# Two mixture-of-experts stages: the first-layer and gate biases move into the weights' last row, and VectorE adds the second-layer bias

## The reference

```python
logits = x @ gate_w.T + gate_b                   # 8 experts
top_vals, top_idx = top_k(logits, 2)
for e in range(8):
    h = x @ w1[e].T + b1[e]                      # 2 x 256 columns
    y = h[:, 0::2] * sigmoid(1.702 * h[:, 0::2]) * (h[:, 1::2] + 1.0)
    out += (y @ w2[e].T + b2[e]) * we[:, None]   # we: routing weight of expert e
```

## Time and profile before

| | |
|---|---|
| runs, us | 1161.66, 1163.23, 1166.33 (median 1163.23) |
| span of the profiled execution, first to last instruction, us | 1142.1 |
| mean granted TensorE clock | 0.931 |
| busy, share of the span | PE 90%, PEld 74%, DVE 64%, ACT 39%, POOL 38% |
| moved by DMA | 72.49 MB, mean 63 GB/s |

### The profile page before, as it was taken

The page is one execution under the profiler, slowest core; times in us unless marked ns, Lnnn a source line. Parts: engine busy times, 40 slices in busy tenths (PEclk is TensorE's granted clock), DMA queues, the critical chain, the costliest instruction groups (busy, mean ns, idle before and its releaser), DMA issues. The chain is left out here.

```text
span 1142.1 us, 18339 instructions
## 1 busy us (share of the span) xinstructions
PE 1029.9 (90%) x6327; PEld 844.4 (74%) x6327; DVE 732.0 (64%) x1755; ACT 449.2 (39%) x768; POOL 430.7 (38%) x473
## 2 busy tenths in 40 slices
PE   4889995879999999978999987999988998899997
PEld 3778884756566655568878886888877987788886
DVE  7935442899788876647454445756648978456654
ACT  4324331327576654525343322232325543232222
POOL 3046663337363721203556531000129987300000
PEclk8689998889899997896999998999998999999999
DMA  9024422400000010119452241000010120000000
GB/s 335 37 74 139 171 88 83 128 0 2 2 2 20 2 39 20 39 37 352 149 189 89 79 174 53 1 1 1 1 74 1 28 47 1 1 1 19 20 19 19
DMA packets 39339, 72.49 MB, mean 63 GB/s; under 512 B 10642, under 2 KB 28114, under 8 KB 38996
## 3 DMA queue, kind: packets, MB, share of 16 engines
q1 hardware_dynamic: 29460, 48.25, 12.6%
q0 software_dynamic: 7680, 20.98, 5.6%
q10 hardware_dynamic: 2112, 2.10, 0.5%
HBM read 47.04 MB, written 24.13 MB: 62 GB/s over the span
## 5 line engine op out<-in xcount | busy, mean ns | idle before, releaser
L2139 PE MATMUL ps<-xt,w 128*128 128x512 f32 x768 | 191.3, 399 | 7.5 <-PEq L66 7.5
L2139 PEld LDWEIGHTS ps<-xt,w 128*128 128x128 f32 x768 | 142.4, 191 | 37.0 <-issue 5.8
L1822 DVE CUSTOM_DVE_ANT_0 ps<-ps,att_mask 128x128 f32<-128x128 f32 (+3 forms) x256 | 119.2, 515 | 27.2 <-PE ps L1371 26.9
L717 PE MATMUL ps<-moe_w,moe_narrow_xb 128*128 x480 | 127.6, 402 | 0.0
L2233 DVE TENSOR_TENSOR had_gated<-ps,had_sig 128x512 f32<-128x512 f32 x64 | 44.2, 691 | 109.7 <-ACT had_sig L2192 109.7
L2192 ACT ACTIVATE had_sig<-ps 128x512 f32<-128x512 f32 x64 | 38.2, 597 | 188.4 <-PE ps L2139 188.4
L1679 ACT ACTIVATE att_early_probs<-ps 128x384 f32<-128x384 f32 (+1 forms) x192 | 91.2, 528 | 52.1 <-PE ps L1386 51.5
L122 POOL TENSOR_TENSOR var_eps<-bn,eps 128x4 f32<-128x4 f32 x24 | 6.6, 274 | 277.0 <-DVE bn L99 263.0
L621 POOL DMA_INDIRECT made_rows<-moe_units_made,moe_index x80 | 79.4, 993 | 80.4 <-ACT moe_units_made L844 68.3
L615 POOL DMA_INDIRECT moe_xs<-xn_rows,moe_index x80 | 79.3, 991 | 76.0 <-DVE moe_index L1016 44.1
L717 PEld LDWEIGHTS ps<-moe_w,moe_narrow_xb 128*128 128x128 f32 x480 | 92.0, 192 | 20.2
(11 more groups left out here) (286 smaller groups left out, 2242.8 us busy)
## 6 DMA issues: line engine op xcount, KB each, us to landing
moe_w<-in_moe SPq DMA_DIRECT2D x16, 768.0 KB, 8.9
back<-made_rows SPq DMA_DIRECT2D x16, 512.0 KB, 5.4
x<-x_turned SPq DMA_DIRECT2D x8, 512.0 KB, 8.6
low_weights<-moe_w SPq DMA_DIRECT2D x4, 768.0 KB, 3.6
moe_w<-low_weights SPq DMA_DIRECT2D x4, 768.0 KB, 15.2
x<-in_x SPq DMA_DIRECT2D x4, 512.0 KB, 5.5
xn_rows<-moe_wide_xn SPq DMA_DIRECT2D x4, 512.0 KB, 10.6
moe_narrow_later<-in_w SPq DMA_DIRECT2D x4, 512.0 KB, 4.6
```

Of the source, the lines that this page charges most:

```text
L717: last = nc.tensor.matmul(h_bank(j, i), xb[a][:, j % 2, i, k, :], weight(c), start=False, stop=(k == KC - 1 and c == 1))
L1822: last = nc.vector.tensor_tensor_reduce(g.ps[:, a, col:col + n], g.ps[:, a, col:col + n], mask[:, SEQ - n:SEQ], -1.0, 3.0e38, ALU.add, ALU ...
L2139: last = nc.tensor.matmul(g.ps[:, bank(n, half), :], w[a][:, k, c * P:(c + 1) * P], xt[low][:, b % 2, k, :], start=(k == 0 and q == 0), st ...
```

## The change

In both expert layers the normalised rows keep 255 columns, and the last is set to 1.0 (by POOL in stage 0; ahead of stage 1 by one small DVE memset for each of the four batches). Since the 256 values add up to zero, the last row of a weight matrix can be subtracted from all the others, and the last row then holds the bias.

- w1: POOL subtracts the last row (broadcast in `w1_last`) from each record, two tensor_tensor of 128 x 512 an expert (`shift_w1`). In stage 0 the last rows are broadcast by four DMAs of 512 KB each (`last_rows`); in stage 1 by products with a column of the identity and four ACT copies.
- b1: PE turns it into `b1_rows`, ACT copies it out, and SP puts row e over the last row of record e by a small DMA (`place_b1`), which waits for the record. `high(e)` waits for the shift and for the placed row.
- Stage 0 shifts all eight experts and stores high and low parts of experts 4 to 7; stage 1 shifts only 0 to 3 and loads both parts of 4 to 7. That is twelve records' worth into SBUF in stage 1, as before.
- gate: `gate_b` becomes the last row of `gate_w`, POOL subtracts the old last row (`shift_gates`); `choose` copies instead of adding.
- b2 is broadcast to all partitions (1 MB), and `out` moves from ACT to DVE: two tensor_tensor of 128 x 256, b2 chosen by a register. `gated` has one buffer instead of two.
- The bias products, `bias_rows` and the tiles for them go away.

The diff, cut:

```diff
+LAST_ROW = slice(REC_W1 - 2 * I, REC_W1)
...
+            def place_b1(e):
+                sp.wait_ge(b1_out, 1)
+                sp.wait_ge(rec_here[e], 16)
+                sp.dma_start(f32(w[1][P - 1:P, e, LAST_ROW]), b1_rows[e:e + 1, :]).then_inc(b1_placed[e], 16)
+            def stored_split(e):
+                sp.dma_start(f32(w[0][:, e, :]), g.split_dram[0, e - E // 2]).then_inc(rec_here[e], 16)
+                sp.dma_start(f32(w[1][:, e, :]), g.split_dram[1, e - E // 2]).then_inc(low_here[e], 16)
+            def last_rows(q):
+                sp.dma_start(w1_last[:, 2 * q:2 * q + 2, :],
+                             ins["moe"][2 * q:2 * q + 2, P - 1, LAST_ROW].partition_broadcast(P)).then_inc(last_here[q], 16)
...
             if which == 0:
...
+                first_biases()
                 for e in range(E // 2):
+                    if e % 2 == 0:
+                        last_rows(e // 2)
                     record(e)
                 for b in range(BATCH):
                     sp.wait_ge(norm.xn_done, b + 1)
                     sp.dma_start(by_tiles(g.xn_dram[:, :], b), g.xn[:, b, :, :]).then_inc(xn_stored, 16)
+                    if b % 2 == 0:
+                        last_rows((E // 2 + b) // 2)
                     record(E // 2 + b)
+                    place_b1(b)
+                for e in range(E // 2, E):
+                    place_b1(e)
+                second_biases()
             else:
+                sp.dma_start(last_row[:, :], ins["moe"][0:OWN, P - 1, LAST_ROW]).then_inc(last_here[0], 16)
+                first_biases()
+                for e in range(OWN):
+                    record(e)
+                for e in range(OWN, E):
+                    stored_split(e)
+                for e in range(OWN):
+                    place_b1(e)
+                second_biases()
...
+                nc.gpsimd.memset(g.xn[:, :, :, D - 1:D], 1.0)
+                norm.rstd(pool, 0)
+                shift_gates()
+                norm.rstd(pool, 1)
+                norm.rstd(pool, 2)
+                shift_w1(0)
+                shift_w1(1)
+                norm.rstd(pool, 3)
+                for e in range(2, E):
+                    shift_w1(e)
...
-                    nc.tensor.matmul(h_bank(j, i), owner_row[:, n:n + 1].to_broadcast([P, P]), b1_row[:, :],
-                                     start=True, stop=False)
...
-                    nc.tensor.matmul(O_BANK[:, i * D:(i + 1) * D], owner_row[:, n:n + 1].to_broadcast([P, P]),
-                                     b2_row[:, :], start=(i == 0), stop=False, skip_group_check=True)
...
             def high(e):
-                act.wait_ge(rec_here[e], 16)
+                act.wait_ge(w1_shifted, e + 1)
+                act.wait_ge(b1_placed[e], 16)
...
                 high_norm(1)
-                high(0)
                 choice.out_of_gates(act, 0, 2)
-                high(1)
+                out_b1(1)
                 high_norm(2)
+                high(0)
                 choice.out_of_gates(act, 1, 3)
+                high(1)
                 high(2)
                 high_norm(3)
...
+            def out(j):
+                mine = [nc.vector.value_load(owner_i[0:1, 2 * j + i:2 * j + i + 1], min_val=0, max_val=E - 1)
+                        for i in range(2)]
+                dve.wait_ge(o_ready, j + 1)
+                if j >= 2:
+                    dve.wait_ge(scattered[j % 2], 32 * (j // 2))
+                for i in range(2):
+                    last = nc.vector.tensor_tensor(made[:, j % 2, i, :], O_BANK[:, i * D:(i + 1) * D],
+                                                   b2[:, bass.ds(mine[i], 1), :], ALU.add)
+                last.then_inc(out_done, 1)
...
                 if 1 <= j <= PAIRS:
                     low_y(j - 1)
+                if j >= 2:
+                    out(j - 2)
                 if 0 <= j - 2 < len(jobs):
                     low_later(j - 2)
```

More of the change, by code:

```diff
@@ L404, in experts_stage @@
         sem = Semaphores(nc, ctx, tag)
-        w = [sb(f"w{q}", [P, E, REC_W1 + REC_W2], F32R) for q in range(2)]
+        w = [sb(f"w{q}", [P, E, REC], F32R) for q in range(2)]
+        b2 = sb("b2", [P, E, D])
         if which == 0:
@@ L462, in experts_stage @@
         xb = [narrow(f"xb{q}", [P, 2, 2, KC, P], F32R) for q in range(2)]
-        gated = narrow("gated", [P, 2, 2, IC, P])
+        gated = narrow("gated", [P, 2, IC, P])
+        sig = narrow("sig", [P, 2, IC, P])
         later = narrow("later", [P, HID])
         consts, small_here, b2_here = sem("consts"), sem("small_here"), sem("b2_here")
+        last_here = [sem(f"last_here{q}") for q in range(4 if which == 0 else 1)]
+        b1_here, b1_turned, b1_out = sem("b1_here"), sem("b1_turned"), sem("b1_out")
+        b1_placed = [sem(f"b1_placed{e}") for e in range(E if which == 0 else E // 2)]
+        last_ps, last_out, w1_shifted, gate_shifted = sem("last_ps"), sem("last_out"), sem("w1_shifted"), sem("gate_shifted")
         x_here = [sem(f"x_here{b}") for b in range(BATCH)]
@@ L635, in _, with turn_b1 @@
         def _(pe):
-            def turn_biases():
-                pe.wait_ge(b1_filled, 1)
+            def turn_b1(bank):
+                pe.wait_ge(b1_here, 16)
                 for q in range(2 * IC):
-                    last = nc.tensor.transpose(Y_BANK[:, q * P:(q + 1) * P], b1_src[:, q, :], g.ident[:, :])
+                    last = nc.tensor.transpose(g.ps[0:E, bank, q * P:(q + 1) * P], b1_all[:, :, q], g.ident[:, :])
                 last.then_inc(b1_turned, 1)
+            if which == 1:
+                turn_b1(LAST_BANKS[0])
+                pe.wait_ge(last_here[0], 16)
+                for e in reversed(range(OWN)):
+                    if e == 0:
+                        pe.wait_ge(b1_out, 1)
+                    nc.tensor.matmul(g.ps[:, LAST_BANKS[e], :], g.ident[0:OWN, e:e + 1].to_broadcast([OWN, P]),
+                                     last_row[:, :], start=True, stop=True).then_inc(last_ps, 1)
             if which == 0:
@@ L683, in _ @@
             if which == 1:
-                pe.wait_ge(lo_split, E - LOADED)
+                pe.wait_ge(lo_split, OWN)
                 spin(nc, g, 4, 6)
-            pe.wait_ge(hi_split, E)
-            pe.wait_ge(lo_split, E - LOADED)
-            if which == 1:
-                for e in range(E - LOADED, E):
-                    pe.wait_ge(low_here[e], 16)
-            pe.wait_ge(b_row, 2)
+            pe.wait_ge(hi_split, OWN)
+            pe.wait_ge(lo_split, OWN)
+            for e in range(OWN, E):
+                pe.wait_ge(rec_here[e], 16)
+                pe.wait_ge(low_here[e], 16)
             pe.wait_ge(owner_done, 1)
@@ L810, in _ @@
                 high(7)
-                high_biases()
                 routes()
             else:
+                out_b1(LAST_BANKS[0])
+                for e in reversed(range(OWN)):
+                    act.wait_ge(last_ps, OWN - e)
+                    nc.scalar.activation(w1_last[:, e, :], g.ps[:, LAST_BANKS[e], :], ACT.Copy).then_inc(last_out, 1)
                 routes()
-                for e in range(E):
+                for e in range(OWN):
                     high(e)
-                high_biases()
                 act.wait_ge(route_turned, 1)
@@ L838, in high_y @@
                 nc.scalar.activation(yb[0][:, j % 2, :, :, :], Y_BANK, ACT.Copy).then_inc(yhi_done, 1)
-            def out(j):
-                act.wait_ge(o_ready, j + 1)
-                if j >= 2:
-                    act.wait_ge(scattered[j % 2], 32 * (j // 2))
-                nc.scalar.activation(made[:, j % 2, :, :], O_BANK, ACT.Copy).then_inc(out_done, 1)
             def high_later(j):
@@ L942, in _ @@
             nc.vector.memset(count[:, 3, :], 1.0)
-            if which == 0:
-                bias_rows()
             padded, ends, starts = count[:, 0, :], count[:, 1, :], count[:, 2, :]
@@ L1024, in _ @@
             dve.wait_ge(routed, 23)
-            nc.vector.tensor_copy(owner_i[:, :], owner[:, :])
-            nc.vector.tensor_scalar(owner_row[:, :], owner[:, :], g.row_e[:, :], None, ALU.is_equal) \
-                .then_inc(owner_done, 1)
-            if which == 1:
-                bias_rows()
-            for e in range(E if which == 0 else 3, E - LOADED):
+            nc.vector.tensor_copy(owner_i[:, :], owner[:, :]).then_inc(owner_done, 1)
+            for e in range(E if which == 0 else 3, OWN):
                 low_weights(e)
```

165 lines of the change are left out of this document (75 added, 90 removed).

## The result

The changed kernel takes 1197.09 us (median of 4 runs, 1190.91 to 1201.79) against 1162.45 of the kernel before beside it: ratio 1.0275, 95% interval 1.0241 to 1.0309. It is **slower by 35 us**, outside the range of the forecast. The profiled execution took 1201.79 us, the slowest of the four; its span is 1199.7.

The account below looks back on a forecast made before the run. Loops were taken as bound by PE's instruction stream, prologues by DMA and the chain through ACT and DVE. Terms -26.1 + 10.1 + 14 + 0.7 = -1.3 gave 1162 us from the median 1163.23; range 1151 to 1171.

Parts of the forecast that it names:

- The loops: Both stages' loops: forty pairs without bias products gain 28.0 us, less 0.5 for POOL and 1.4 for a stall: -26.1.
- the 5.08: Both loops: forecast period of one pair in us without the bias products, down from 5.78.
- what I had named as able to take over: Loops at the new period: POOL's transfers (5.1 us a pair), DVE (4.2) or PE's wait for `low_x` (0.27 away).
- The stall for later weights: Stage 1's loop: ACT's 4.64 us stand for a transfer of later weights grows, giving 1.4 us back.
- POOL's 5.1 a pair: Loops: POOL's four indirect transfers take 5.1 us a pair, level with PE; 0.5 us taken off the gain.
- Stage 0's prologue: Before stage 0's loop: broadcasts delay record 6 and b1's placement, so the last choice ends at 47.7 against 37.58, +10.1 us.
- my chain: Stage 0's prologue: after ACT's 1.48, DVE's three splits, one low part and four choices run without a gap, 10.8 us.
- the upper bound: Stage 0's prologue: +14 us if the chain's three splits each stood behind one POOL shift, +3.6.
- Stage 1's prologue: Before stage 1's loop: b1 placements queue behind all twelve records in SP's queue, delaying the third split and index, +14 us.
- Overtaking: Faster rival, chance 0.20: placements overtake the records, stage 1's prologue loses 7 instead of 14 us; 1155, or 1149.
- DVE's output step: Slower rival, chance 0.12: register loads make DVE bind the loops at about 5.5 us a pair; 1177 us.
- Free products: Rival, chance 0.03: in the loops PE would wait elsewhere for the same time, so only losses stay; 1188 us.

Follow-up runs that it names:

- second trace of before: The kernel before, unchanged, profiled once more: one run, 1167.07 us, span 1165.3.
- the two experiments on it: Changed kernel with the output step back on ACT as a copy without b2, 1197.19 us; with expert 0's b2 and no DVE register loads, 1205.97 us.

## Why the prediction was wrong

**The loops: -26.1 forecast, +2.3 measured. This is the step that failed**, in two places.

- *"the median of the runs, 1163.23, lies 21.1 above it, and I take that difference as it is."* The sum stood on an execution that isn't an ordinary one. The profile after, and every other one here, has its whole time some 2 us above its span; 21 us were a warning that the trace lacked something, and I had passed it by. What it lacked are the held signals of PE. They are in both kernels and come with the indirect transfers: plain ones of the same size take 29 us from the one and 32 to 38 from the other. The pairs shown, in which ACT gets its signal about 4 us late, aren't bound by PE's products. How an indirect transfer holds a signal of PE, and why the first trace went without, no run shows.
- *"So the loops are bound by PE's instruction stream, and a product left out there is worth its distance, not its duration."* True of the products, not of what else stands in that queue. I priced PE's register loads at 0.30 each for DVE and never asked whether they lay hidden on PE. Under twenty-eight products they all but did (0.9 us of "issue"); under twenty-four they don't (9.7). With plain transfers the four products are worth 5.6 us, and 19.8 more in the loops come by taking the loads out (stage 0's loop then also ran at a granted clock of 1.00 instead of 0.96). With both out of the way the pair is 5.05 us, so the price of a product fits. It is no proof of the 5.08: that was to be had with the loads and the indirect transfers in place.

Added up from the windows of single executions: without held signals and PE's register loads -25.4, against a kernel before that still has its loads; the loads give 19.8 back; and the held signals take 34.8 us from the loops after, against 26.9 in the second trace of before, 7.9 more. That makes the +2.3. So the loads on PE ate most of the gain, not the held signals, which both kernels pay; and the 7.9 is little more than executions of one loop differ by (stage 0's alone took 136.8 to 142.3).

Of what I had named as able to take over, none decided. DVE leaves a pair its 5.05 us with the output step in place. The stall for later weights grew as forecast in direction: ACT stands 6.92 us ahead of 617.16, 31 us after the stage's first product, where the earlier trace rows have 4.64. That is 2.3 more, in a trace with held signals; I had put 1.4. POOL's 5.1 a pair wasn't put to the test, since no kernel with all its indirect transfers came down to that.

**Stage 0's prologue: +10.1 forecast, +18.0 measured; the term was mis-sized.** The direction and the carrier were right: record 6 isn't in place by 31 (it is issued at 30.79), and the roundings wait for placed rows; but the last choice was to lie at 45 to 50. The row placed in record 2 was to let ACT go on at 35.4 and does so at 41.35, 6.0 later; and ACT stands once more, for the row of record 3, until 46.87, where my chain ran on without a wait: 2.3 more. Three things that delay these rows are missing in the sum: the gate's load, which I had seen as a wait and judged covered; the collision of POOL and DVE, which I kept for the upper bound and put on the splits (they take 1.74 to 1.84 mostly) when it strikes the normalisations; and SP's own wait at the first placement, with stores and records queued behind it. What each is worth stays open, since the runs on them moved the last choice by little more than executions without any edit there differ. By the same spread the +18.0 is the high end: the first product comes at 81.26 to 84.55 in the seven executions with this prologue, against 66.57.

**Stage 1's prologue: +14 forecast, +17.5 measured; right in its mechanism, with a second limit overlooked.** The placements do queue behind the records (26.6 us after the margin, forecast 25.7; the 0.6 for the small transfer's own landing came from no row). What I called covered, the products for the last rows, isn't: they end long before the placed rows land, but the ranking stands behind them and comes 9.2 us later, and the subtraction stretches DVE's small steps. Taking the ranking ahead alone gave 1.9 us, with early placements 7.6. Early placements alone weren't run; that the index would then have come almost as late is an estimate from the 9.2 and the stretched steps.

**The rivals.** *Overtaking* fell by the wait of 13.63. *DVE's output step* fell by the two experiments on it, though its sign came true by another way (1177 for it, 1197 measured). *Free products* came nearest: 1188 for "only the losses stay", and the losses were 11 us larger. I gave it 0.03 on the strength of a gapless pair, in a trace that lacked the gaps; without held signals and with the loads in place the products were worth 5.6 us, near nothing indeed. Even with a gain of 26 us the prologues would have made it 1163 - 26 + 18 + 17.5 + 0.7 = 1173, slower and outside the range.

## What to carry to other kernels

Before a sum is built on a trace, compare its span with the timed runs: a span that is 2% short is of another execution than the one you are asked about, and the difference lies inside it until a second trace says otherwise. When a gapless engine is relieved of work, list everything else in its queue, register loads too, and ask what of it was hidden by what you remove. An order by hand on three queues costs more than its transfers: each step put ahead of an old one (a load that delays the issue behind it, a wait in SP's queue, products ahead of the ranking) is to be priced by what stands behind it.

## What the runs showed of the hardware

- Beside indirect transfers from POOL, ACT's copy started 4.64 us (before) and 3.68 us (after) past the end of the product's record in the pairs shown; with plain ones of the same size, or with the gathers left out, its list has no such start. POOL's part of a transfer also falls, from 0.96 to 0.54 us, so POOL's time and the kind of transfer aren't told apart.
- After such a stall twelve products took 5.48 us at a granted clock of 0.5, against 2.96 in a pair without.
- PE's four register loads a pair: without them the two loops with plain transfers were 19.8 us shorter, and PE's "issue" waits of 9.7 us ahead of its first group were gone.
- The issue behind a load of 127 rows took 5.24 us on SP's queue; behind loads of 112 and 15 rows, 1.19 together, it took 0.22.
- Four DVE normalisations of 128 x 255 took 4.24 us beside POOL's subtractions, 5.16 when they met them 1.1 us earlier, and 1.38 without; steps of 128 x 8 took 1.1 instead of 0.17.
